# GpSimd's gathers and scatters of a mixture-of-experts layer dealt out over all expert steps, with eight gather buffers

## The reference

```python
w_topk, idx_topk = jax.lax.top_k(gates, TOPK)            # 8 of 64 experts for a token
...
rank = jnp.arange(A) - starts[se]
valid = rank < CAPACITY                                  # 160 rows for each expert
buf = jnp.zeros((NUM_EXPERTS, CAPACITY, H)).at[se, rank].set(x[st], mode='drop')
h = jnp.einsum('ech,efh->ecf', buf, expert_w1)           # 160 x 128 by 128 x 768
x1, x2 = jnp.split(h, 2, axis=-1)
out = jnp.einsum('ecf,ehf->ech', x1 * jax.nn.silu(x2), expert_w2)
y = jnp.where(valid[:, None], out[se, clip(rank)] * sw[:, None], 0.0)
combined = jnp.zeros((T, H)).at[st].add(y)
```

## Time and profile before

| | us |
|---|---|
| median of 3 runs | 721.71 |
| the three runs | 721.12, 721.71, 726.26 |
| the profiled execution, its own time | 723.01 |
| its span, from first to last instruction | 721.2 |
| PE busy | 580.0 |
| DVE busy | 453.1 |
| POOL busy | 345.1 |

### The profile page before, as it was taken

The page is one execution under the profiler, slowest core; times in us unless marked ns, Lnnn a source line. Parts: engine busy times, 40 slices in busy tenths (PEclk is TensorE's granted clock), DMA queues, the critical chain, the costliest instruction groups (busy, mean ns, idle before and its releaser), DMA issues.

```text
span 721.2 us, 11097 instructions
## 1 busy us (share of the span) xinstructions
PE 580.0 (80%) x3755; PEld 479.8 (67%) x3755; DVE 453.1 (63%) x1362; ACT 230.2 (32%) x434; POOL 345.1 (48%) x341
## 2 busy tenths in 40 slices
PE   7998878668987787797999035789999999999960
PEld 5767655668977776797995024567787778778640
DVE  4678768943424322333433787887877787777994
ACT  3142234002322212222332011224344444443664
POOL 4656101873566666576444488343322332342352
PEclk9999997879999999999999556799999999999995
DMA  8960001126666766676716900000000000000001
GB/s 298 415 260 23 16 7 36 45 72 203 209 222 200 231 220 190 190 237 218 239 61 213 398 2 0 0 12 5 15 26 4 15 15 11 4 30 0 1 1 59
DMA packets 29564, 79.42 MB, mean 110 GB/s; under 512 B 7104, under 2 KB 12096, under 8 KB 29264
## 3 DMA queue, kind: packets, MB, share of 16 engines
q1 hardware_dynamic: 23088, 65.69, 26.3%
q0 software_dynamic: 6432, 13.16, 6.0%
HBM read 62.60 MB, written 16.25 MB: 109 GB/s over the span
## 4 chain that ended last, share of the span: by engine, by line
PE 58%; DVE 23%; issue 8%; another core or an unknown queue 4%; POOL 2%; ACT 2%; DMA 1%; SPq 0%; DVEq 0%; ACTq 0%; POOLq 0%
PE bank L780 13%; PE bank L946 6%; PE bank L790 6%; PE bank L934 6%; PE bank L539 4%; PE bank L876 3%; PE bank L894 2%; DVE stats L256 2%; DVE arena L1659 2%; PE bank L857 2%; PE bank L871 2%; DVE hidden L1743 2%; PE bank L885 2%; PE bank L912 2%
## 5 line engine op out<-in xcount | busy, mean ns | idle before, releaser
L271 POOL TENSOR_TENSOR rstd<-veps,minus_half 128x4 f32<-128x4 f32 x52 | 54.0, 1039 | 209.9 <-DVE veps L264 208.4
L780 PE MATMUL bank<-hidden,ring 128*128 128x160 f32 x768 | 123.4, 311 | 4.6 <-issue 2.7
L780 PEld LDWEIGHTS bank<-hidden,ring 128*128 128x128 f32 x768 | 113.4, 200 | 6.5 <-issue 4.3
L1347 POOL DMA_INDIRECT returned_rows<-x1t,scatter_all x80 | 79.3, 991 | 65.9 <-DVE x1t L1754 21.8
L1153 ACT ACTIVATE hidden<-bank 128x480 f32<-128x480 f32 x64 | 36.9, 576 | 177.6 <-PE bank L780 110.5
L790 PE MATMUL bank<-hidden,ring 128*128 128x160 f32 x384 | 66.4, 310 | 31.8 <-DVE hidden L1743 19.1
L790 PEld LDWEIGHTS bank<-hidden,ring 128*128 128x128 f32 x384 | 56.0, 193 | 37.3 <-DVE hidden L1743 22.8
L1731 DVE COPY hidden<-bank 128x384 f32<-128x384 f32 (+1 forms) x32 | 22.9, 719 | 66.3 <-PE bank L780 33.9
L1211 ACT ACTIVATE arena<-bank,layer_cols 128x512 f32<-128x512 f32 x64 | 44.0, 687 | 62.6 <-PE bank L934 62.6
L946 PE MATMUL bank<-ring,arena 128*128 128x128 f32 x512 | 59.9, 275 | 1.4 <-issue 1.4
L946 PEld LDWEIGHTS bank<-ring,arena 128*128 128x128 f32 x512 | 58.4, 192 | 2.4 <-issue 2.4
(11 more groups left out here) (222 smaller groups left out, 1156.9 us busy)
## 6 DMA issues: line engine op xcount, KB each, us to landing
ring<-in_ew SPq DMA_DIRECT2D x64, 576.0 KB
returned_rows<-zeros SPq DMA_DIRECT2D x16, 512.0 KB, 14.6
arena<-returned_rows SPq DMA_DIRECT2D x6, 512.0 KB, 12.7
hidden<-returned_rows SPq DMA_DIRECT2D x4, 512.0 KB, 5.0
ring<-returned_rows SPq DMA_DIRECT2D x4, 512.0 KB, 8.6
ring<-in_l1w SPq DMA_DIRECT2D x8, 256.0 KB, 2.6
returned_rows<-x1t,scatter_all POOLq DMA_INDIRECT x80
shared<-in_xr SPq DMA_DIRECT2D x1, 1024.0 KB, 8.3
```

What stands on the lines that cost most here:

```text
L271: pool.tensor_tensor(rstd[:, s, :], veps[:, s, :], minus_half[:], ALU.pow).then_inc(sem(f"rstd{which}_ready"), 1)
L780: mm = pe.matmul(bank[2 * (n % 2) + part][:, CAP * f:CAP * f + CAP], ring[:, n % RING, P * (FB * part + f):P * (FB * part + f) + P], E["xt ...
L1347: pool.indirect_dma_start(returned_dram[:, :], bass.IndirectOffsetOnAxis(ap=scatter_all[:, Q, b:b + 1], axis=0), E["back"][:, Q % BACK, b, ...
```

## The change

- There are eight gather buffers in place of four. The four new ones lie in the memory of the low one-hot tables of groups 0 to 3, which `find_slots` has read by then. For that the tables are stored group by group: the group becomes the outer dimension, in VectorE's writes (line 1659) and in TensorE's reads (line 736). With eight buffers a gather waits for slot gates only from group 8 on, and for those of group Q - 8.
- GpSimd's order is new. Twenty gathers (groups 0 to 3) come first. In each of steps 0 to 7 two blocks are gathered. From step 8 to step 51 each step issues its scatters of group (n - 8) // 4, one, one, two and one of them in turn, and then one gather. From step 52 on the scatters come as two, two, one and none. The last scatter of group 14 and the five of group 15 close it.
- Four semaphores are saved, to make room for the four of the new buffers: the ones of early loads are counted on for the encoder layers' weights. The waits ask for one more count of 16; the loads and their order stay.
- The loads of the returned rows, and all that follows, are as before.

The diff, its core (the other renamed semaphores follow the same pattern):

```diff
@@ -202,7 +202,7 @@
         slot_gate = sb("slot_gate", [NEG, RB])
         picked_gate = sb("picked_gate", [RB, EG])
         TE = TILES * NE
-        R = carve([("a", (TILES, NEG * RA * EG), F16), ("b", (2 * RB, TE), F16), ("mask", (TE,), F16)])
+        R = carve([("a", (NEG, TILES, RA * EG), F16), ("b", (2 * RB, TE), F16), ("mask", (TE,), F16)])
         at_mask = (RA * TE + 2 * RB * TE) // 2
         ai16, bi16 = zeros[:, 0:TE // 2].bitcast(F16), zeros[:, TE // 2:TE].bitcast(F16)
 
@@ -220,9 +220,10 @@
         bq_up = sb("bq_up", [LAYERS])
         den1, rden1 = sb("den1", [2, GT, HEADS]), sb("rden1", [2, GT, HEADS])
 
-        GOT, BACK = 4, 3
+        GOT, BACK = 8, 3
         got_at = [arena[:, at_mask:at_mask + RB * ROUTED], logits[:].rearrange("p i e -> p (i e)")[:, 0:RB * ROUTED],
                   gates[:].rearrange("p i e -> p (i e)")[:, 0:RB * ROUTED], small[:, 0:RB * ROUTED]]
+        got_at += [arena[:, TILES * RA * EG // 2 * q:TILES * RA * EG // 2 * q + RB * ROUTED] for q in range(GOT - 4)]
         got = [a.rearrange("p (b c) -> p b c", c=ROUTED) for a in got_at]
         E = {"back": x1t[:, 0:BACK * RB * D].rearrange("p (u b c) -> p u b c", u=BACK, b=RB)}
         flat_hidden = hidden[:].rearrange("p a n -> p (a n)")
...
-            sp.dma_start(cols(xt, 1), cols(xt0, 1)).then_inc(sem("second_xt_in"), 16)
+            sp.dma_start(cols(xt, 1), cols(xt0, 1)).then_inc(sem("second_xt_then_qkv_in"), 16)
...
-            a16 = R["a"].rearrange("p i (g n) -> p i g n", n=RA * EG)
+            a16 = R["a"]
...
-                            mm = pe.matmul(slot_bank(call)[:, at:at + 2 * RB * EG], a16[:, i, 2 * q + u, :],
+                            mm = pe.matmul(slot_bank(call)[:, at:at + 2 * RB * EG], a16[:, 2 * q + u, i, :],
...
-                pe.wait_ge(sem("qkv_in"), 16 * (l + 1))
+                pe.wait_ge(sem("second_xt_then_qkv_in"), 16 * (l + 2))
...
@@ -1349,30 +1350,28 @@
                                         E["back"][:, Q % BACK, b, :], None, bounds_check=TOK * TOPK - 1,
                                         oob_is_err=False).then_inc(sem(f"scattered{Q % BACK}"), 16)
 
-            AHEAD = 6
+            BEFORE, FIRST_SCATTER = 4, 2 * EG
+
+            def gather_blocks(first, count):
+                for k in range(first, min(first + count, NEG * RB)):
+                    gather_block(k // RB, k % RB)
+
             pool.wait_ge(sem("rows_out"), 16 * 2 * GROUPS)
-            for Q in range(AHEAD):
-                for b in range(RB):
-                    gather_block(Q, b)
+            gather_blocks(0, BEFORE * RB)
             pool.wait_ge(sem("zeroed"), 16 * TOK * TOPK // (8 * P))
-            def step(n):
-                pool.wait_ge(sem("expert_mm"), min(n + 1, NE + LAG))
-
-            for Q in range(NEG):
-                n = EG * Q + 2 * EG
-                step(n)
-                for b in (0, 1):
-                    scatter_block(Q, b)
-                step(n + 1)
-                for b in (2, 3, 4):
-                    scatter_block(Q, b)
-                if Q + AHEAD < NEG:
-                    step(n + 2)
-                    for b in (0, 1):
-                        gather_block(Q + AHEAD, b)
-                    step(n + 3)
-                    for b in (2, 3, 4):
-                        gather_block(Q + AHEAD, b)
+            for n in range(NE + LAG):
+                pool.wait_ge(sem("expert_mm"), n + 1)
+                if n < FIRST_SCATTER:
+                    gather_blocks(BEFORE * RB + 2 * n, 2)
+                else:
+                    Q = (n - FIRST_SCATTER) // EG
+                    gathering = BEFORE * RB + FIRST_SCATTER + n < NEG * RB
+                    for b in (((0,), (1,), (2, 3), (4,)) if gathering else ((0, 1), (2, 3), (4,), ()))[n % EG]:
+                        scatter_block(Q, b)
+                    gather_blocks(BEFORE * RB + FIRST_SCATTER + n, 1)
+            scatter_block(NEG - 2, RB - 1)
+            for b in range(RB):
+                scatter_block(NEG - 1, b)
 
 
             def row_of(l, k):
-            a_out = R["a"].rearrange("p i (g a e) -> p i g a e", a=RA, e=EG)
+            a_out = R["a"].rearrange("p g i (a e) -> p g i a e", e=EG)
...
-                ins = v.tensor_tensor(a_out[:, first:last, Q],
+                ins = v.tensor_tensor(a_out[:, Q, first:last],
...
```

More of the change, by code:

```diff
@@ L428, in _ @@
             sp.dma_start(C[:, 0:C_BLK], cst[:, 0:C_BLK]).then_inc(sem("first_consts_in"), 16)
[L429 to L430 removed]
+            sp.dma_start(cols(xt, 1), cols(xt0, 1)).then_inc(sem("second_xt_then_qkv_in"), 16)
+            sp.dma_start(w0[:, W_O:], l0w[:, W_O:]).then_inc(sem("wo_then_o_in"), 16)
             sp.dma_start(xr[:], xr0).then_inc(sem("xr_in"), 16)
[L432 to L433 removed]
+            sp.dma_start(xt[:, 2 * GROUP:], xt0[:, 2 * GROUP:]).then_inc(sem("xt_then_up_in"), 16)
+            sp.dma_start(sw[:], l0s).then_inc(sem("sw_then_down_in"), 16)
             sp.dma_start(C[:, C_BLK:], cst[:, C_BLK:]).then_inc(sem("consts_in"), 16)
@@ L467, in _ @@
                 sp.dma_start(spare[i], mine[i]).then_inc(sem(f"returned_in{i // GT}"), 16)
-            sp.dma_start(w_up, l1w[0][:, 4 * P:8 * P]).then_inc(sem("up_in"), 16)
-            sp.dma_start(w_down, l1w[0][:, 8 * P:12 * P]).then_inc(sem("down_in"), 16)
+            sp.dma_start(w_up, l1w[0][:, 4 * P:8 * P]).then_inc(sem("xt_then_up_in"), 16)
+            sp.dma_start(w_down, l1w[0][:, 8 * P:12 * P]).then_inc(sem("sw_then_down_in"), 16)
             sp.dma_start(mod_sb, mod_w).then_inc(sem("mod_in"), 16)
@@ L475, in _ @@
                 sp.wait_ge(sem("kv1_mm"), 2 * GROUPS * l)
-                sp.dma_start(w_qkv, w[:, 0:3 * P]).then_inc(sem("qkv_in"), 16)
+                sp.dma_start(w_qkv, w[:, 0:3 * P]).then_inc(sem("second_xt_then_qkv_in"), 16)
                 sp.wait_ge(sem("out1_mm"), GROUPS * l)
-                sp.dma_start(w_o, w[:, 3 * P:4 * P]).then_inc(sem("o_in"), 16)
+                sp.dma_start(w_o, w[:, 3 * P:4 * P]).then_inc(sem("wo_then_o_in"), 16)
                 sp.wait_ge(sem("up_mm"), FFB * GROUPS * l)
-                sp.dma_start(w_up, w[:, 4 * P:8 * P]).then_inc(sem("up_in"), 16)
+                sp.dma_start(w_up, w[:, 4 * P:8 * P]).then_inc(sem("xt_then_up_in"), 16)
                 sp.wait_ge(sem("down_mm"), GROUPS * l)
-                sp.dma_start(w_down, w[:, 8 * P:12 * P]).then_inc(sem("down_in"), 16)
+                sp.dma_start(w_down, w[:, 8 * P:12 * P]).then_inc(sem("sw_then_down_in"), 16)
             for g in range(GROUPS):
@@ L495, in project_first @@
                 if g == 1:
-                    pe.wait_ge(sem("second_xt_in"), 16)
+                    pe.wait_ge(sem("second_xt_then_qkv_in"), 16)
                 if g == 2:
-                    pe.wait_ge(sem("xt_in"), 16)
+                    pe.wait_ge(sem("xt_then_up_in"), 16)
                 if g:
@@ L589, in attention_out @@
                 if g == 0:
-                    pe.wait_ge(sem("wo_in"), 16)
+                    pe.wait_ge(sem("wo_then_o_in"), 16)
                 pe.wait_ge(sem("an_ready"), g + 1)
@@ L614, in route_logits @@
                 if g == 0:
-                    pe.wait_ge(sem("sw_in"), 16)
+                    pe.wait_ge(sem("sw_then_down_in"), 16)
                 pe.wait_ge(sem("x1t_ready"), g + 1)
@@ L904, in output @@
             def output(n, k, g, l):
-                pe.wait_ge(sem("o_in"), 16 * (l + 1))
+                pe.wait_ge(sem("wo_then_o_in"), 16 * (l + 2))
                 pe.wait_ge(sem("at_ready"), n + 1)
@@ L924, in up @@
             def up(n, k, g, l):
-                pe.wait_ge(sem("up_in"), 16 * (l + 1))
+                pe.wait_ge(sem("xt_then_up_in"), 16 * (l + 2))
                 pe.wait_ge(sem("h2t_ready"), n + 1)
@@ L937, in down @@
             def down(n, k, g, l):
-                pe.wait_ge(sem("down_in"), 16 * (l + 1))
+                pe.wait_ge(sem("sw_then_down_in"), 16 * (l + 2))
                 pe.wait_ge(sem("relu_ready"), FFB * (n + 1))
```

7 lines of the change are left out of this document (2 added, 5 removed).

## The result

The changed kernel takes 714.5 us (median of four, 713.17 to 716.08), the kernel before 721.4 on the same chip; the ratio is 0.9885, with a 95% interval of 0.984 to 0.993. The forecast was 701, in a band of 693 to 714 and a whole range of 681 to 728; the measured time is just above the band and inside the range. Its profiled execution took 713.17 us with a span of 711.4, so the two profiled executions differ by 9.8 us and the medians by 6.9; what follows accounts for the spans.

The account below looks back on a forecast made before the run. TensorE was taken as the longest engine, losing 47 us to late reports beside runs of indirect DMAs. From 723.0 us, 22.2 for steps 8 to 51 and 0 for all else gave 701 us, range 681 to 728.

Parts of the forecast that it names:

- What bounds the kernel: Expert steps: TensorE is the longest engine, but its reports come late beside long runs of indirect DMAs; 47 us can be touched.
- Steps 8 to 51: Main expert steps: 99 indirect DMAs in place of 105, priced at 1.41 us each, 139.6 us, a gain of 22.2.
- the middle: Price for each DMA in steps 8 to 51: 1.41 us, between 1.28 (GpSimd never waiting) and 1.54 (old pace).
- Steps 0 to 7: First eight expert steps: some 20 DMAs, priced 0, with 2 us of gain and 3 of loss as bounds.
- Lead of the gathers: Group 15's last gather, due in step 51 and needed in step 57, still fits; priced 0.
- Steps 52 on: Last expert steps, last ten scatters, the return and the rest: same order and count, priced 0.
- Tables: Eleven table writes of 12.7 us before the steps: new layout priced 0, with 1.3 us either way as bound.
- GpSimd's durations: GpSimd's indirect DMAs in the expert steps should stay at 0.96 us a gather and 0.99 a scatter.
- The gather beside the table writes: Before the expert steps: a gather takes 1.96 us beside VectorE's table writes, 0.95 alone; no sign of it in expert steps.
- Reports on time: Rival, chance 0.22: gathers in a run alone hold reports, so GpSimd's queue bounds the steps; 37 us less, 686 us.
- A toll for each DMA: Rival, chance 0.22: every indirect DMA beside matmuls costs 1.5 us wherever it stands, so redistribution does nothing; 723 us.
- No pause to recover: Rival, chance 0.17: late reports catch up only when GpSimd idles; without idle stretches 52 steps cost 3.78 us each; 731 us.

Follow-up runs that it names:

- e2: The changed kernel without the 40 gathers of groups 8 to 15, which are computed from old rows; 684.9 us.
- e4: The changed kernel with the 40 gathers of groups 8 to 15 replaced by 40 memsets on GpSimd at the same places; 682.1 us.
- e1: The changed kernel with its eight buffers, table layout and semaphores, but GpSimd's old schedule; 729.9 us, ratio 1.0138 to the kernel before.
- e9: The changed kernel with a memset of 128x128 floats behind each indirect DMA from the 21st to the 150th; about the changed kernel's time.
- e11: The changed kernel with a memset of 128x256 floats behind each indirect DMA from the 21st, none behind the last ten scatters; ratio 0.981 to the kernel before.
- e7: The changed kernel with the 44 gathers of its steps 8 to 51 spread over steps 8 to 54; 712.2 us, ratio 0.9877 to the kernel before.
- e17: The changed kernel with the 40 gathers of groups 8 to 15 cut to 64 of 128 rows, on a chip that holds reports; 713.4 us.
- e3: The changed kernel with the 40 gathers of groups 8 to 15 replaced by plain DMAs of the same bytes issued by SyncE; 686.1 us.
- e8: The changed kernel with the 40 gathers of groups 8 to 15 replaced by plain DMAs issued by GpSimd in the same places; 681.3 us.

## Why the prediction was wrong

- **What bounds the kernel.** Right: late reports of TensorE beside GpSimd's indirect DMAs, worth about 47 us in all. On the chip where four other kernels show none, the kernel before is 43.8 us quicker (721.4 - 677.6); no profile of it was taken there. e2 to e4 confirm 2.73 us a step as TensorE's own pace.
- **Steps 8 to 51, the step that failed.** The text priced the 99 DMAs at 1.41 us, "the middle", and so had a gain of 22.2. They took 1.53, the upper bound of 1.54 almost exactly, and the gain was 10.3. The middle had no row of its own: it supposed that without runs of five gathers fewer reports would be late. 15 of 44 were, where 17 had been. e1 and e9 to e11 show that the pace hardly moves: 1.52 to 1.54, whether GpSimd issues every 1.29 or every 1.49 us, and in either order, while the late reports go from 13 to 26. A row that pointed there was at hand: steps with ten DMAs took 15.1 to 15.2 us each time. So steady a number should have been the value and not the bound. It is a rate over many steps only: in the changed kernel four steps take 10.0 to 16.3 us, 1.43 to 1.69 for each DMA.
- **Steps 0 to 7.** Priced 0 with 2 us of gain as a bound; measured 2.3. 20 DMAs were priced there, 17 ran, at 1.48 (25.2 / 17). e1 shows what was missed: the holes of the earlier trace rows also let TensorE's reports through. In the kernel before those of steps 2 and 5 come inside the two holes, at 167.13 and 176.07 us; e1 has no first hole, and step 2's waits until the second. With the eight buffers it is the new waits, a report for every two gathers, that set this stretch apart from e1's 35 us.
- **Lead of the gathers.** 0, right: TensorE waits for none. e7 found where it ends: three steps later TensorE waits 2.9 us.
- **Steps 52 on.** Priced 0, measured 2.6 us of loss: DMAs that slid past step 51, 19 instead of 15. Tables 0: eleven writes still take 12.7 us, as in the earlier trace rows. GpSimd's durations: 0.98 to 1.00 against 0.96 to 0.99, so 1 to 3% up, which the pace hides.
- **The gather beside the table writes** was misread, without effect on the sum. The 0.95 us taken for a gather alone, at 144.09 us in the earlier trace rows, runs beside a table write too (144.07 to 145.35 us); those that start 0.07 us after a table write's start, as at 145.34, take 1.96. The gathers without a table write, from 149.88 us on, take 0.95 as well. The table writes are f16 TENSOR_TENSORs with both inputs in SBUF, 1.22 us each; no run varies them, and the expert steps show nothing of the kind.
- **Reports on time** (686) was wrong on every chip that holds them; on the one that does not, no report was late, but the changed kernel itself was not timed.
- **A toll for each DMA** (723) had the mechanism: 1.5 us wherever it stands. e17 adds that it is a toll on the DMA, not on rows. Its time was wrong because it counted to step 51 only. The old order left time at both ends in which no DMA paid it, 15 DMAs in 27.5 us and 15 in 32.5; the new one has 17 in 25.2 and 19 in 35.1. From the first expert matmul to the last step's report both have 135 POOL instructions, the old one in 221.8 us and the new one in 211.8: that is the whole gain. The Trainium skill (DMA: Bandwidth & Descriptors, section Queues, rings and completion order) has the DMA engines take turns between queues by the packet; e3, with more bytes and no late report, speaks against the toll being paid there.
- **No pause to recover** (731) was right for what it named, and wrong as a sum: with unbroken gathers e1 ends at 729.9, but the new order has GpSimd wait for each step, and that wait is the pause. That e1 comes so near 731 is luck: it loses its time in the first eight steps, and its steps 8 to 51 take 160.7 us, no more than before.

What makes TensorE's report wait is open. Shown are: in these steps it goes with GpSimd's indirect DMAs, 98 to 105 of them in 44 steps at 1.29 to 1.49 us from start to start, and all but ends at 60 of them or at 1.55 us; VectorE's reports pass meanwhile; in the kernels before and after, 31 of 36 held reports (over 2 us, those right behind another left out) come in a pause of GpSimd, 0.1 to 2.6 us after its last DMA's end, but the others in the middle of a run, as do most of e11's; and all this is absent on one chip of five. A plain queue that lets a report through once the DMAs issued before it are served does not give the measured lateness: in e1 step 1's report passes in the middle of a run at 162.72 us and step 2's at 174.70, though GpSimd issued only two DMAs between the ends of the two steps' matmuls. Whether the change does anything on the chip without late reports was not timed.

## What to carry to other kernels

When a stalling stretch takes the same time in every period, divide it by what it issues and price the change at that rate, over the whole stretch up to both ends (here 1.53 us for each indirect DMA); a reordering then gains only where it fills time in which the rate was not used. Count the waits that a change removes as something that others may live on: here a hole in GpSimd's queue let TensorE's reports through, and eight buffers without a new order cost 8 us. And run the kernel before on more than one chip before tuning against a stall of this kind: 1.55 us between DMAs ends the late reports and takes 2% less than the kernel before on one chip, as 1.49 us does without ending them, and costs 4% on another.

## What the runs showed of the hardware

- TensorE's semaphore increments can be held back for up to 12.2 us (e1) while GpSimd issues indirect DMAs back to back; ScalarE, VectorE and SyncE then see them at the same moment (174.70 us in e1), and VectorE's increments are not held (0.05 to 0.06 us in 19 waits of the changed kernel).
- With 86 to 105 indirect DMAs in steps 8 to 51, they never went below 1.50 us of time for each on four chips, at spacings from 1.29 to 1.55 us; on a fifth a spacing of 1.25 to 1.29 was kept up for 44 steps. A scatter (0.98 us there, 0.99 to 1.00 elsewhere) and twelve matmuls (1.80) take nearly the same there, and the kernel before takes 677.6 us against 720.6 to 724.8.
- A gather of 64 rows keeps GpSimd 0.91 to 0.92 us (e17) where 128 rows keep it 0.99 (the changed kernel); a plain DMA of the same 128 rows issued by GpSimd takes it 0.59 (e8).
